# Attention scores from whole float32 q and k, four heads in four 32-row tiles

## The reference, cut to what matters

```python
def _binarize(W):                       # one factor for each output row, times the signs
    return mean(|W|, axis=1) * sign(W)
def _binlinear(x, W, b):
    return einsum('btc,oc->bto', x, _binarize(W)) + b

h = layernorm(x)
q, k, v = (split_heads(_binlinear(h, W, b)) for W, b in ((Wq, bq), (Wk, bk), (Wv, bv)))
att = softmax(einsum('bhtd,bhsd->bhts', q, k) * 16 ** -0.5)
y = einsum('bhts,bhsd->bhtd', att, v)   # heads put together again
x = x + layernorm(_binlinear(y, Wp, bp))
# feed-forward on the new x, 256 -> 1024 -> 1024 -> 1024 -> 256:
h = silu(lin(n, w1)) * lin(n, w2); h = gelu(lin(h, h1)); h = gelu(lin(h, h2))
x = x + layernorm(lin(h, w3))           # n is the layernorm of x
```

## Time and profile before

| | |
|---|---|
| time, median of 3 runs | 1378.12 us |
| the profiled execution, its span | 1376.7 us |
| TensorE busy | 1267.2 us (92%) |
| ScalarE busy | 810.4 us (59%) |
| VectorE busy | 586.3 us (43%) |
| GpSimd busy | 76.8 us (6%) |
| first score matmul, last p·v matmul start | 140.9 us, 661.8 us |
| mean granted TensorE clock | 0.966 of 2.4 GHz |

### The profile page before, as it was taken

One profiled execution on the slowest core, in us unless ns is written; L12 is line 12 of the kernel. 1 busy time (PEld: TensorE's weight loads), 2 busy tenths in 40 slices (PEclk: granted clock), 3 DMA queues, 4 the chain that ended last, 5 costly groups with the idle time before them and its releaser, 6 DMA issues.

```text
span 1376.7 us, 19093 instructions
## 1 busy us (share of the span) xinstructions
PE 1267.2 (92%) x6696; PEld 743.3 (54%) x6696; DVE 586.3 (43%) x1012; ACT 810.4 (59%) x928; POOL 76.8 (6%) x36
## 2 busy tenths in 40 slices
PE   2774999999999999997499999998999989999997
PEld 2652222222222222221288888887888878888886
DVE  7994011111111111104465574755747647476523
ACT  3784899999999999996333423424234242243411
POOL 5465000000000000000000000000000000000000
PEclk9996899999999999998699999999999999999999
DMA  3679766677777766681200010100100001010000
GB/s 119 205 220 281 163 120 120 138 130 128 128 128 128 150 140 119 119 164 37 62 1 31 1 62 1 31 32 2 61 1 31 32 2 61 1 31 1 0 16 16
DMA packets 60438, 110.60 MB, mean 80 GB/s; under 512 B 6114, under 2 KB 31074, under 8 KB 60330
## 3 DMA queue, kind: packets, MB, share of 16 engines
q1 hardware_dynamic: 60372, 109.72, 34.7%
HBM read 75.73 MB, written 45.48 MB: 88 GB/s over the span
## 4 chain that ended last, share of the span: by engine, by line
PE 49%; DVE 1%; issue 1%; ACT 0%; DVEq 0%; ACTq 0%
PE ffn_ps L1155 22%; PE ffn_ps L1156 22%; PE ffn_ps L1183 2%; PE ffn_ps L1184 2%; PE side_ps L1139 1%; PE side_ps L1148 1%; DVE ln_stats L1290 0%; DVE zn L1301 0%; DVE zn L1342 0%; DVE x L1325 0%; DVE x_lo L1332 0%; DVE zn L1318 0%; DVE zn L1315 0%; DVE zn L1352 0%; DVE ln_mean_var L1294 0%
## 5 line engine op out<-in xcount | busy, mean ns | idle before, releaser
L931 ACT ACTIVATE probs<-s_ps 128x1024 f32<-128x1024 f32 x512 | 495.9, 1021 | 32.9 <-PE s_ps L899 26.5
L1156 PE MATMUL ffn_ps<-h_lo,W 128*128 128x512 f32 x1024 | 401.5, 392 | 0.0
L1155 PE MATMUL ffn_ps<-h_hi,W 128*128 128x512 f32 x1024 | 401.5, 392 | 0.0
L883 PE MATMUL y_ps<-probs,v_st 128*32 128x512 f32 x2048 | 274.3, 608 | 9.9 <-DVE y_sb L968 9.2
L899 PE MATMUL s_ps<-q_st,k_st 99*128 99x512 bf16 x1024 | 270.9, 385 | 11.3 <-issue 10.4
L899 PEld LDWEIGHTS s_ps<-q_st,k_st 99*128 99x128 bf16 x1024 | 78.7, 98 | 292.3 <-ACT probs L931 220.7
L1246 ACT ACTIVATE hid<-ffn_ps,scales 128x512 f32<-128x512 f32 x128 | 81.1, 686 | 232.9 <-PE ffn_ps L1156 228.0
L1156 PEld LDWEIGHTS ffn_ps<-h_lo,W 128*128 128x128 f32 x1024 | 192.5, 188 | 42.2
L1155 PEld LDWEIGHTS ffn_ps<-h_hi,W 128*128 128x128 f32 x1024 | 192.5, 188 | 42.2
L960 DVE TENSOR_SCALAR low_bits<-W 128x1408 int32 (+1 forms) x16 | 14.3, 893 | 305.1 <-DMA W<-w_scr 305.1
L1366 DVE CAST h_hi<-hid 128x512 fp32r<-128x512 f32 x128 | 53.4, 417 | 185.1 <-ACT hid L1246 184.8
(11 more groups left out here) (105 smaller groups left out, 1029.3 us busy)
## 6 DMA issues: line engine op xcount, KB each, us to landing
q_st<-q_scr SPq DMA_DIRECT2D x96, 128.0 KB, 6.8
k_st<-k_scr SPq DMA_DIRECT2D x96, 128.0 KB, 7.1
w_scr<-ffn_w SPq DMA_DIRECT2D x16, 704.0 KB, 13.5
W<-w_scr SPq DMA_DIRECT2D x16, 704.0 KB, 12.4
v_scr<-v_aug SPq DMA_DIRECT2D x8, 1024.0 KB, 4.3
v_st<-v_scr SPq DMA_DIRECT2D x16, 512.0 KB, 11.5
y_scr<-y_sb SPq DMA_DIRECT2D x16, 512.0 KB, 3.3
q_scr<-part SPq DMA_DIRECT2D x24, 256.0 KB, 4.5
```

Source lines behind the costliest of these rows:

```text
L883: i = pe.matmul(y_ps[32 * j:32 * (j + 1), tb * BLK:(tb + 1) * BLK], v_st[u][:, s, 32 * j:32 * (j + 1)], probs[s % 2][j][:, tb * BLK:(tb + ...
L931: act.activation(probs[s % 2][j][:, :], s_ps[a % 3][:, :], ACT.Exp, scale=SCALE).then_inc(probs_ready, 1)
L1155: pe.matmul(bank_of(t)[:, :], w, hi[:, k, :].bitcast(form), start=(k == 0), stop=False)
L1156: mm = pe.matmul(bank_of(t)[:, :], w, lo[:, k, :].bitcast(form), start=False, stop=last)
```

## The change

q and k stay whole, in float32. The splitting into parts goes: `high_of_qk`, `mid_of_qk`, `rest_of_qk` and GpSimd's subtraction. `copy_qk` now waits for the stores of block n-2, because q and k are stored from its output; the squares are taken of the whole q and k. Each block has 2 stores of 512 KB for q and k in place of 6 of 256 KB.

A quad's q is one tile of 128 rows x 1024, and so is its k: head j has rows 32j to 32j+15, and row 32j+16 is the shift in q and one in k. It takes 8 loads of 64 KB, one for v and 4 one-row loads of the shift. A score matmul has 17 rows, in the row tile at 32j. A score buffer now holds 512 queries of two heads, and so does an exponential; their number and shape stay. The loops go over halves of the queries outside and stretches of keys inside; p·v of a group (one stretch, one half, four heads) follows two score steps, one group later. Each half of y is copied when it is complete. At the start of the tail's blocks, ScalarE and VectorE wait for the last store of y.

```diff
-def load_stacks(sp, q_scr, k_scr, q, k, g, done, groups=range(6)):
-    for i in groups:
-        at = slice(i * HEAD_DIM, (i + 1) * HEAD_DIM)
-        for st, scr, s in ((q, q_scr, Q_PART[i]), (k, k_scr, K_PART[i])):
-            sp.dma_start(st[at, :, :], scr[s, bass.ds(g * QROWS, QROWS), :]
-                         .rearrange("(j d) t -> d j t", d=HEAD_DIM)).then_inc(done, 16)
+def load_heads(sp, q_scr, k_scr, q, k, g, done, heads=range(QUAD)):
+    for j in heads:
+        at = slice(j * STRIP, j * STRIP + HEAD_DIM)
+        for st, scr in ((q, q_scr), (k, k_scr)):
+            sp.dma_start(st[at, :], scr[bass.ds(g * QROWS + j * HEAD_DIM, HEAD_DIM), :]).then_inc(done, 16)
...
-                for u in range(2):
-                    sp.dma_start(quads.q[u][STACK:STACK + 1, :, :],
-                                 shift[u * QUAD:(u + 1) * QUAD, :]).then_inc(quads.m_loaded[u], 16)
-                for s, src in enumerate((shift, zeros, zeros)):
-                    sp.dma_start(m_scr[s], src[:, :]).then_inc(shift_stored, 16)
+                for u in range(2):
+                    for j in range(QUAD):
+                        at = j * STRIP + HEAD_DIM
+                        sp.dma_start(quads.q[u][at:at + 1, :], shift[j:j + 1, :]).then_inc(quads.m_loaded[u], 16)
+                sp.dma_start(m_scr[:, :], shift[:, :]).then_inc(shift_stored, 16)
...
-                    for s, (done, credit) in enumerate(((high_done, 0), (mid_done, 0), (low_done, 1))):
-                        if s == 1 and loads:
-                            sp.wait_ge(norm_done, TILES * (n + 3))
-                            load(n + 4, u)
-                        sp.wait_ge(done, credit + n + 1)
-                        for scr, m in ((q_rows, 0), (k_rows, CT)):
-                            sp.dma_start(scr[s, b, :, :, u * BLK:(u + 1) * BLK],
-                                         part[s][u][:, m:m + CT, :]).then_inc(stored[u], 16)
+                    sp.wait_ge(qk_copied, QK * (n + 1))
+                    for scr, m in ((q_rows, 0), (k_rows, CT)):
+                        sp.dma_start(scr[b, :, :, u * BLK:(u + 1) * BLK], qk[u][:, m:m + CT, :])\
+                            .then_inc(stored[u], 16)
+                    if loads:
+                        sp.wait_ge(norm_done, TILES * (n + 3))
+                        load(n + 4, u)
...
             def copy_qk(b, u, n, tiles):
-                if not is_first(n):
-                    act.wait_ge(rest_done, n)
+                act.wait_ge(stored[u], 16 * (STORES * b + 1))
...
+            def scores(g, u, a):
+                tb, s, pp = a // (ST * PAIRS), a // PAIRS % ST, a % PAIRS
+                pe.wait_ge(probs_ready, g * N + ((2, 3, 1)[a] if a < 3 else a + 1))
+                for hh in range(2):
+                    at = (2 * pp + hh) * STRIP
+                    i = pe.matmul(s_ps[a % 3][:, hh, :], k_st[u][at:at + HEAD_M, s * P:(s + 1) * P],
+                                  q_st[u][at:at + HEAD_M, tb * BLK:(tb + 1) * BLK], start=True, stop=True,
+                                  tile_position=(at, 0))
+                i.then_inc(scored, 1)
+            def pv(g, u, m):
+                tb, s = divmod(m, ST)
+                pe.wait_ge(probs_ready, 3 + g * N + PAIRS * (m + 1))
                 for j in range(QUAD):
                     i = pe.matmul(y_ps[32 * j:32 * (j + 1), tb * BLK:(tb + 1) * BLK],
                                   v_st[u][:, s, 32 * j:32 * (j + 1)],
-                                  probs[s % 2][j][:, tb * BLK:(tb + 1) * BLK],
+                                  probs[m % 2][j // 2][:, j % 2, :],
                                   start=(s == 0), stop=(s == ST - 1), tile_position=(0, 32 * j))
                 i.then_inc(pv_done, 1)
...
+                for m in range(GROUPS):
+                    scores(g, u, 2 * m)
+                    scores(g, u, 2 * m + 1)
+                    if m:
+                        if (m - 1) % ST == 0 and not (start and m == 1):
+                            pe.wait_ge(y_copied, 2 * g + (m - 1) // ST)
+                        pv(g, u, m - 1)
+                    elif not start:
+                        pv(g - 1, 1 - u, GROUPS - 1)
...
+                    for m in range(GROUPS):
+                        act.wait_ge(pv_done, g * GROUPS + m + 1)
+                        for pp in range(PAIRS):
+                            a = m * PAIRS + pp
                             act.wait_ge(scored, g * N + a + 1)
-                            act.activation(probs[s % 2][j][:, :], s_ps[a % 3][:, :], ACT.Exp,
+                            act.activation(probs[m % 2][pp][:, :, :], s_ps[a % 3][:, :, :], ACT.Exp,
                                            scale=SCALE).then_inc(probs_ready, 1)
...
                     for tb in range(2):
-                        dve.wait_ge(pv_done, 4 + 2 * (g + 1) * ST - 1 + tb)
+                        dve.wait_ge(pv_done, 2 + g * GROUPS + (tb + 1) * ST)
...
+            for u in range(2):
+                act.wait_ge(tail_in.y_stored[u], 16 * (QUADS // 2 + 1))
             blocks(act, step, end)
```

More of the change, by code:

```diff
@@ L48 @@
 QROWS = QUAD * HEAD_DIM
-STACK = 6 * HEAD_DIM
-STACK_M = STACK + 3
+STRIP = 32
+PAIRS = QUAD // 2
+HEAD_M = HEAD_DIM + 1
 EPS = 1e-5
@@ L213, in layer @@
         quads = Quads(
-            q=[right(f"q_st{u}", [STACK_M, QUAD, SEQ], BF16) for u in range(2)],
-            k=[right(f"k_st{u}", [STACK_M, QUAD, SEQ], BF16) for u in range(2)],
+            q=[right(f"q_st{u}", [P, SEQ], F32) for u in range(2)],
+            k=[right(f"k_st{u}", [P, SEQ], F32) for u in range(2)],
             v=[right(f"v_st{u}", [P, ST, P], F32) for u in range(2)],
@@ L434, in _ @@
                 body(b, True)
-            body(BATCH - 2, False, (range(0, 3), range(3, 6)))
+            body(BATCH - 2, False, (range(0, 2), range(2, 4)))
             body(BATCH - 1, False)
             for u in range(2):
-                sp.wait_ge(quads.m_loaded[u], 16)
+                sp.wait_ge(quads.m_loaded[u], 16 * QUAD)
         @block.vector
@@ L551, in _ @@
                                channel_multiplier=-1).then_inc(filled, 1)
-            for s in (low_done, rest_done, norms_done, norms_read):
+            for s in (norms_done, norms_read):
                 pool.sem_inc(s, 1)
@@ L561, in _ @@
             for u in range(2):
[L562 to L565, removed]
+                pool.memset(quads.k[u][:, :], 1.0).then_inc(bound_set, 1)
+                pool.memset(quads.q[u][:, :], 0.0).then_inc(bound_set, 1)
             pool.wait_ge(small_loaded, 16 * 5)
@@ L570, in _ @@
                     n = 2 * b + u
-                    pool.wait_ge(mid_done, n + 1)
-                    pool.wait_ge(stored[u], 16 * (STORES * b + 1))
-                    pool.tensor_tensor(part[2][u][:, :, :], rest[u][:, :, :], part[1][u][:, :, :],
-                                       ALU.subtract).then_inc(low_done, 1)
                     pool.wait_ge(v_scaled, n + 1)
@@ L757, in attention @@
         N = QUAD * ST
-        probs = [[sb(f"probs{w}{j}", [P, SEQ], F32) for j in range(QUAD)] for w in range(2)]
+        GROUPS = 2 * ST
+        probs = [[sb(f"probs{w}{pp}", [P, 2, BLK], F32) for pp in range(PAIRS)] for w in range(2)]
         y_sb = [sb(f"y_sb{u}", [P, SEQ], F32) for u in range(2)]
@@ L761, in attention @@
         row_top = sb("row_top", [P, N], F32)
-        neg = [sb(f"neg{s}", [N, P], F32) for s in range(3)]
-        m_part = sb("m_part", [N, 3, P], BF16)
-        s_ps = [ctx.enter_context(nc.psum_tensor(f"s_ps{i}", [P, SEQ], F32)) for i in range(3)]
+        neg = sb("neg", [N, P], F32)
+        s_ps = [ctx.enter_context(nc.psum_tensor(f"s_ps{i}", [P, 2, BLK], F32)) for i in range(3)]
         y_ps = ctx.enter_context(nc.psum_tensor("y_ps", [P, SEQ], F32))
@@ L787, in _, with load_shift @@
         def _(sp):
+            def load_shift(g, u, done):
+                for j in range(QUAD):
+                    at = j * STRIP + HEAD_DIM
+                    sp.dma_start(q_st[u][at:at + 1, :], m_scr[bass.ds(g * QUAD + j, 1), :]).then_inc(done, 16)
             wide = sp.value_load(const.wide_range[:, :], min_val=0, max_val=1)
@@ L791, in _ @@
                     sp.wait_ge(stored[u], 16 * (STORES * BATCH + 1))
-                sp.wait_ge(quads.shift_stored, 48)
+                sp.wait_ge(quads.shift_stored, 16)
                 sp.wait_ge(loaded[0], 16 * QUAD_LOADS)
@@ L891, in quad @@
                 pe.wait_ge(loaded[u], 16 * QUAD_LOADS * (h + 1))
-                pe.wait_ge(m_loaded[u], 16 * (h + 1))
-                for s in range(ST):
-                    for j in range(QUAD):
-                        a = s * QUAD + j
-                        pe.wait_ge(probs_ready, g * N + ((2, 3, 1)[a] if a < 3 else a + 1))
-                        for tb in range(2):
-                            i = pe.matmul(s_ps[a % 3][:, tb * BLK:(tb + 1) * BLK],
-                                          k_st[u][:, j, s * P:(s + 1) * P],
```

(13 more changed lines are left out.)

113 lines of the change are left out of this document (36 added, 77 removed).

## The result

The changed kernel takes 1802.47 us in the median of 4 runs (1798.09 to 1803.7), the kernel before 1378.53 us beside it (1377.88 to 1379.54). The ratio is 1.3067, with a 95% interval of 1.3049 to 1.3086: 424 us more, where 15 were forecast and the range ended at 1468 us.

The account below looks back on a forecast made before the run. It took TensorE to bind attention, by 0.12 us a group over the exponentials. Attention +46.8, quad 14 -5 and projection -27 gave +15: a span of 1391.7 us, 1393 as median, range 1350 to 1468.

Parts of the forecast that it names:

- the price of a pass: Attention: float32 score passes in four row tiles run side by side and cost what p·v does, 854 ns of streaming.
- quad 14: Attention's one longer quad, 41.1 us where 31.9 were due, TensorE restarting at clock 0.50; forecast to gain some 5 us.
- rivals 2: Attention scores: row tiles load weights one after another, 0.3 to 0.7 us in each group, 1465 to 1561 us; chance 13%.
- 3 (strict order): Attention scores: passes start strictly in order, five steps of 0.427 in place of two, about 1690 us; chance 8%.
- the two-tile case: Attention scores: only two tiles run side by side, 2.9 to 3.0 us a group, some 1585 us; chance 2%.
- The scores' 0.98 us: Attention, each group: eight score passes take 0.10 exposed load + 0.854 streaming + 0.02 = 0.98 us.
- The stagger of 0.08: Attention: every other score step waits 0.08 us for an exponential's buffer, so a group takes 2.16 us, not 2.08.
- Rival 1: Attention: weight load hidden and second pair not held up, 1.99 to 2.06 us a group, 1362 us at 2.03; chance 27%.
- The sign: Whole kernel: slower 0.61, faster 0.32, same 0.07.
- Projection: Stage before attention: 9.3 us a block in place of 12.79, with block 0 and the stage's end -27 us together.
- The loop's own cost: Attention: 0.015 us added to each group, from 1.98 - 1.965.
- the attention term: Attention: 15 quads x 16 groups x (2.16 + 0.015 - 1.98) = +46.8 us, before quad 14's -5.

Follow-up runs that it names:

- e1: The changed kernel with score matmuls of 32 rows a tile in place of 17, the added rows holding zeros in q and ones in k: 1372.7 us.
- e5: The changed kernel with score matmuls of 32 rows a tile instead of 17, timed in 6 runs: 1372.06 us in the median, ratio 0.9942 to the kernel before.
- e4: The changed kernel, still with 17-row scores, with one full-array matmul of 512 columns added in each group of attention: 1475.39 us.
- e7_half_exp: The changed kernel with 32 rows a tile, each exponential from the third quad on covering only 256 of each head's 512 columns: 1344.11 us.
- e8_gpsimd: The changed kernel with 32 rows a tile, GpSimd working on a spare float32 tile in each projection block with nobody waiting for it: 1378.23 us.
- e2_before17: The kernel before with its bf16 score matmuls cut from 99 rows to 17: 1799.41 us.

## Why the prediction was wrong

**The step that failed** is the price of a pass, "Side by side in four tiles the price is that of p·v, 854 ns of streaming", and with it "p·v's 0.91". 427 ns a pass was read in rows where the granted clock was 1.00, and was carried over to a group in which the rows of the scores had been changed from 99 to 68. The clock's lower level in steady attention stood only as the last item of what would show the forecast wrong, without a mechanism, a price or a chance. Its price was in the rows: the restart of quad 14 shows a p·v burst of 1.93 us at 0.50. A burst of scores is about as long as one of p·v (0.98 and 0.91 us at the upper level), so at the lower one a group would have been about 3.9 us; by the measured 3.89, 256 x (3.89 - 2.16) = +443 us on the forecast's 1393. With 17 us more gained in the projection and 10 in the tail that is 1809, against 1802 measured. What the runs showed in its place: with 17 rows a tile every pass of attention, p·v's too, ran at 0.50; with 32 rows (e1, e5) at 1.00, at the price forecast.

That the clock follows the rows in use could have been asked, not known: before is at 0.98 from 140 to 640 us with 99 rows, and its attention has no stretch with fewer. The Trainium skill (TensorE: Matmul & The Clock Gate, Part 3, the table of speedups) gives row tiles of 32 rows as a gain alone, 3.07 times; e5_rows32_timed agrees on the gain (eight passes of 0.43 us within 1.14), and the changed kernel shows, with 17 rows in each tile, a clock that takes back more than it.

**What was right, shown with the clock up** (e1, e5; for 17 rows e4, where p·v follows the scores' start by 1.07 us as well). Four row tiles run side by side, two passes each: rivals 2 (loads one after another), 3 (strict order) and the two-tile case are wrong, at either level. The Trainium skill's strict order of starts and ends (same page and part, The mechanism) would give five steps only if each head's two passes followed each other in the program; the records start in fours instead (in e5_rows32_timed from 404.34 and from 404.87 us), and which order the passes have in the program no row shows, so the runs rule out the staircase and not the page's sentence. The scores' 0.98 us: in e7_half_exp they begin 1.07 us before p·v, which is 0.98 and 0.09 for the change of form. TensorE's need of 2.08 a group: 2.07. The stagger of 0.08 and its cause: 2.07 and 2.23 in turn, gone with shorter exponentials. Rival 1 (load hidden) is wrong, as the 0.10 is there. The sign was right in the changed kernel, but not for the reason given: with the clock up the time is 0.6% under before, so +15 would have been wrong too.

**Terms of the sum that were mis-sized**, beside the clock. Projection: -27, measured -44 (-45 in e1_rows32); 9.3 us a block was 8.0. The normalisations fell to 1.38 us in all blocks but the first, the case that the prediction names ("5.9 if the normalisation is freed as well") but didn't take; e8_gpsimd puts 8 to 9 us on it. In the regular steps of 7.6 to 7.7 us TensorE is then busy throughout at 1.00; the forecast had left it 9.6 and 8.8 us of work, read at 0.87 and 0.93. The DMA engines are nearly full in the same stretch, so no slack is left there either. The new wait on the stores, priced at nothing, did hold ScalarE, 9.8 us in five waits; TensorE worked on through the short ones, and the longest, 4.79 us, stands in the step of 10.5. The loop's own cost: 0.015 a group, measured 35.35/16 - 2.15 = 0.06, some 10 us in all. It is mostly not the loop's: with half exponentials 33.26/16 - 2.07 = 0.01 is left, and the rest is the wait at the quad's step. Quad 14, priced at 5 us: in e1_rows32 no wait of TensorE is left there, of 9.2 before. With the clock up the attention term holds: from first score to last p·v e5_rows32_timed takes 567.9 us, 46 more than before, where 46.8 - 5 = 42 were forecast. Projection and tail turn the sum's sign.

The tail, priced at nothing, is 10 us shorter in the changed kernel (9.7 in e1_rows32, 8.5 in e5). Its waits tell a part (columns: who waited for what, us in total, times, longest), before and then after:

```profile
PE ffn_ps L1155 <- issue: 8.2, 4, 2.4
```

```profile
PE ffn_ps L1096 <- issue: 2.4, 1, 2.4
```

The same matmuls of unchanged code stood four times for nothing that the profile shows, and afterwards once. Why isn't settled; e5_rows32_timed has two such waits, and in e4_fill1, which has the changed kernel's tail too, the tail takes 714 us as before. So these 10 us can't be put down to the change.

## What to carry to other kernels

Before a matmul is cut to fewer rows, ask what it does to the granted clock of everything around it: here a kernel that fed 68 rows at once where 99 had worked before ran all of its attention at 1.2 GHz, and padding the same tiles with zeros to 32 rows each gave 430 us back, at no cost in time: at 1.00 eight score passes take 1.14 us with 17 rows (e4_fill1) and with 32. Read a duration together with the granted clock of its stretch, and price each forecast at both levels when the change touches what TensorE does per unit of time. And look at an untouched operation first: p·v's 608 to 1061 ns told at once that this was the clock and nothing in the changed lines.

## What was not expected of the hardware

- Rows that multiply zeros count: the 15 rows added to each tile hold q = 0, and the clock rose from 0.50 to 1.00.
- Busy is not enough: TensorE was busy for 500 of 500 us at 0.50 in the changed kernel, with float32 scores in row tiles, and for 498 in e2_before17, with bf16 scores in one tile. The Trainium skill (TensorE: Matmul & The Clock Gate, Part 1) ties the clock to how busy TensorE has been of late. For the time at work that rule and these rows differ, and the rows decide; the idle gap before attention (0.50 from 87 to 97 us) agrees with it.
- 32 rows in one tile (1800 us) and in four (1373 us) differ as 17 and 99 do.
- One VectorE operation (128x256 or 64x1024, in e8_gpsimd) can last as long as a GpSimd pass over 128x2048 float32 that runs beside it: 2.74 us where 0.41 is usual, and 3.92 where 0.76 is.
